# A graph layer's edge kernel on one core: second layer's units behind the repeat, gates reordered, node table in three pieces, start and end written out

## The reference

```
r    = edge_vec / |edge_vec|                                      # 3 numbers; sh1 = sqrt(3) * r
xs, xd = x[src], x[dst]                                           # gather
s1 = 16 scalars, v1 = 16 vectors of both
w  = relu(emb @ fc1_w1 / sqrt(10)) @ fc1_w2 / 4                   # 512 weights of this edge
s_t, v_t = tensor product of (s1, v1, sh1) with w                 # 8 scalars, 8 vectors
w2 = relu(emb @ fc2_w1 / sqrt(10)) @ fc2_w2 / 4                   # 384 weights of this edge
scal, gates, vecs = tensor product of (s_t, v_t, sh1) with w2
edge_out = [tanh(scal), vecs * tanh(gates)] * norm                # 32 numbers
```

## Time and profile before

| what | us |
|---|---|
| median of 3 runs (784.5 to 785.16) | 785.0 |
| the profiled execution | 785.59 |
| its span, first to last instruction | 783.4 |
| VectorE busy | 728.3 (93%) |
| TensorE busy | 672.7 (86%) |
| ScalarE busy | 552.9 (71%) |
| GpSimd busy | 536.4 (68%) |
| largest group: L728 x104, 2290 ns each | 238.2 |
| next: L690 x104, 2289 ns each | 238.1 |

### The profile page before, as it was taken

The page is one execution under the profiler, slowest core; times in us unless marked ns, Lnnn a source line. Parts: engine busy times, 40 slices in busy tenths (PEclk is TensorE's granted clock), DMA queues, the critical chain, the costliest instruction groups (busy, mean ns, idle before and its releaser), DMA issues.

```text
span 783.4 us, 20601 instructions
## 1 busy us (share of the span) xinstructions
PE 672.7 (86%) x6667; PEld 306.0 (39%) x6770; DVE 728.3 (93%) x1321; ACT 552.9 (71%) x1279; POOL 536.4 (68%) x655
## 2 busy tenths in 40 slices
PE   0788889999998999899998999899999998999874
PEld 0533434443444444343444434344444434443323
DVE  8389999999999999999999999999999999999964
ACT  2267777777777777877787777777777777777731
POOL 8577877688767877687768776887688767876100
PEclk9699999999999999999999999999999999999998
DMA  3321111111111111111112111111111111111000
GB/s 103 92 61 21 45 28 38 24 43 27 39 28 44 28 25 37 44 28 28 40 24 44 26 39 24 47 28 39 21 45 28 34 28 37 27 25 24 11 1 22
DMA packets 36099, 27.34 MB, mean 35 GB/s; under 512 B 14326, under 2 KB 34448, under 8 KB 35994
## 3 DMA queue, kind: packets, MB, share of 16 engines
q1 hardware_dynamic: 21646, 18.15, 8.1%
q0 software_dynamic: 13312, 6.84, 5.9%
q10 hardware_dynamic: 1036, 1.02, 0.4%
HBM read 21.77 MB, written 4.20 MB: 33 GB/s over the span
## 4 chain that ended last, share of the span: by engine, by line
PE 60%; DVE 29%; issue 7%; DMA 1%; ACT 1%; POOL 0%; DVEq 0%; SPq 0%; POOLq 0%
DVE z_s L728 13%; PE ps L957 12%; PE ps L894 10%; PE ps L878 8%; DVE p_s L690 7%; PE ps L937 6%; PE ps L866 4%; PE ps L912 4%; PE ps L858 3%; PE ps L885 3%; PE ps L950 2%; PE ps L925 2%; PE ps L944 2%; PE ps L968 1%; DMA x_dram<-eo_all 1%
## 5 line engine op out<-in xcount | busy, mean ns | idle before, releaser
L335 POOL DMA_INDIRECT xs<-in_xp,src_i x416 | 405.4, 974 | 111.7 <-issue 105.5
L728 DVE TENSOR_TENSOR z_s<-ps,h 128x2048 f32<-128x2048 f32 x104 | 238.2, 2290 | 10.5 <-PE ps L912 1.2
L690 DVE TENSOR_TENSOR p_s<-ps,h 128x2048 f32<-128x2048 f32 x104 | 238.1, 2289 | 5.9 <-PE ps L957 5.9
L483 ACT CAST v_s<-ps 128x512 bf16<-128x512 f32 x312 | 181.4, 581 | 48.6 <-PE ps L878 45.3
L957 PE MATMUL ps<-f,w_f 32*128 32x512 f32 x832 | 120.5, 645 | 50.3 <-DVE z_s L728 32.0
L878 PE MATMUL ps<-p_s,sum_m 128*32 128x512 f32 x832 | 110.8, 601 | 15.3 <-DVE m L744 8.4
L894 PE MATMUL ps<-z_s,w_z 128*32 128x512 f32 x832 | 110.8, 605 | 3.8 <-DVE z_s L728 2.5
L446 ACT COPY oht<-ps 42x512 bf16<-42x512 bf16 x104 | 60.3, 580 | 68.6 <-PE ps L858 68.6
L377 POOL TENSOR_TENSOR along<-fe,r 128x192 f32<-128x192 f32 x104 | 58.6, 564 | 56.7 <-ACT fe L464 50.7
L452 ACT COPY f<-ps 128x512 f32<-128x512 f32 x104 | 61.0, 586 | 41.1 <-PE ps L866 41.1
L937 PEld LDWEIGHTS ps<-ident,u 128*128 128x128 f32 x416 | 43.6, 140 | 86.4 <-issue 86.4
(11 more groups left out here) (115 smaller groups left out, 890.8 us busy)
## 6 DMA issues: line engine op xcount, KB each, us to landing
emb<-e_dram SPq DMA_DIRECT2D x309, 30.0 KB
xs<-in_xp,src_i POOLq DMA_INDIRECT x416
e_dram<-e_part SPq DMA_DIRECT2D x7, 360.0 KB, 3.2
e_in<-in_emb SPq DMA_DIRECT2D x8, 240.0 KB
window<-x_dram SPq DMA_DIRECT2D x104, 7.9 KB
x_dram<-eo_all SPq DMA_DIRECT2D x1, 585.9 KB
eo_all<-in_vec_t SPq DMA_DIRECT2D x1, 528.0 KB, 3.6
xt_n<-in_xt SPq DMA_DIRECT2D x1, 400.0 KB, 3.7
```

Source lines behind the costliest of these rows:

```text
L335: nc.gpsimd.indirect_dma_start(xs_r[n][:, t, :], None, xp, bass.IndirectOffsetOnAxis(src_i[:, m * T + t:m * T + t + 1], axis=0)).then_inc( ...
L483: nc.scalar.copy(v_s[:], v_ps).then_inc(v_step, 1)
L690: nc.vector.tensor_tensor(p_s[:], ps[:, 0:4, :], h1_r[m % 2][:].unsqueeze(1).to_broadcast([128, 4, BE]), ALU.mult).then_inc(p_done, 1)
L728: nc.vector.tensor_tensor(z_s[:], ps[:, 0:4, :], h2_r[k % 3][:].unsqueeze(1).to_broadcast([128, 4, BE]), ALU.mult).then_inc(z_done, 1)
```

## The change

- Order on PE and ACT: hidden_2(i+1) at the end of step i becomes hidden_2(i) in step i, on PE behind repeat(i-1) and ahead of sum_1(i), on ACT first of all.
- `gates`: m4 first, then m1, then the addition to m4.
- Node table: `x_dram` is (3, N + 42, 32) instead of (N + 42, 96); each part is stored when ready, by a DMA of its own; a window load has 126 rows of 64 bytes instead of 42 of 192.
- Start: the misfits copy on DVE right after the first weight copy; turn_one_hot(0) one step earlier; the keep_warm(8) at i = -3 gone; tile 3 of block 1's and tile 0 of block 2's gather behind the branch on the flag.
- End: STEPS ends at NB; what remains of the last four blocks is written out. There over_nodes also waits for accumulate of the block before, and the keep_warm calls are 2, 4 and 4 instead of 4, 8, 8 and 4.

```diff
-        x_dram = nc.dram_tensor("x_dram", (N + WIN, PARTS * D), BF16, kind="Internal").ap()
+        x_dram = nc.dram_tensor("x_dram", (PARTS, N + WIN, D), BF16, kind="Internal").ap()
...
-        STEPS = range(-5, NB + 6)
+        STEPS = range(-5, NB + 1)
...
-                sp.dma_start(window_r[m % 3][:], x_dram[bass.ds(base, WIN), :].rearrange("m (n c) -> m n c", n=PARTS)
+                sp.dma_start(window_r[m % 3][:], x_dram[:, bass.ds(base, WIN), :].rearrange("n m c -> m n c")
                              ).then_inc(window_loaded[m % 3], 16)
...
-            sp.wait_ge(x_part_ready, PARTS)
-            sp.dma_start(x_dram[0:N, :].rearrange("(p m) c -> p m c", p=P), x_part.rearrange("p m n c -> p m (n c)")
-                         ).then_inc(x_stored, 16)
+            for n in range(PARTS):
+                sp.wait_ge(x_part_ready, n + 1)
+                sp.dma_start(x_dram[n, 0:N, :].rearrange("(p m) c -> p m c", p=P), x_part[:, n, :, :]).then_inc(x_stored, 16)
...
-            gather(1, 0, T)
-            gather(2, 0, 1)
+            gather(1, 0, 3)
             pool.wait_ge(r4_ready, 1)
             pool.wait_ge(misfits_ready, 1)
...
+                        if i == -4:
+                            gather(1, 3, T)
                         if real(i + 3):
                             directions(i + 3)
                         if i == -3:
-                            gather(2, 1, T)
+                            gather(2, 0, T)
...
             for i in STEPS:
+                if real(i):
+                    hidden_2(i)
                 if real(i):
                     part_of_v(i, 0)
...
                 if real(i - 4):
                     copy_one_hot(i - 4)
-                if real(i + 1):
-                    hidden_2(i + 1)
                 later_emb(i)
...
+            copy_one_hot(NB - 3)
+            tanhs(NB - 2)
+            copy_one_hot(NB - 2)
+            tanhs(NB - 1)
+            copy_one_hot(NB - 1)
...
             link(nc.vector.tensor_copy(w_first[:], w1_s))
+            dve.wait_ge(misfit_sum, 1)
+            nc.vector.tensor_copy(misfits[:], ps[0:1, 7, 0:1]).then_inc(misfits_ready, 1)
             link(nc.vector.tensor_tensor(w1_s, w1_s, w_first[:], ALU.subtract))
...
-                r = r4[:, T * k:T * k + T, :].unsqueeze(3).to_broadcast([128, T, 4, 16])
-                nc.vector.tensor_tensor(m1[:], e_ps[:, :, :, 0:16], r, ALU.mult).then_inc(fin_step, 1)
                 r = r4[:, T * k:T * k + T, 1:4].unsqueeze(3).to_broadcast([128, T, 3, 8])
                 nc.vector.tensor_tensor(m4[:], e_ps[:, :, 0:1, 16:24].to_broadcast([128, T, 3, 8]), r,
                                         ALU.mult).then_inc(vec_step, 1)
+                r = r4[:, T * k:T * k + T, :].unsqueeze(3).to_broadcast([128, T, 4, 16])
+                nc.vector.tensor_tensor(m1[:], e_ps[:, :, :, 0:16], r, ALU.mult).then_inc(fin_step, 1)
                 dve.wait_ge(vec_step, k + 1)
...
+            a, b, c, d = range(NB - 4, NB)
+            gates(c)
+            gated(b)
+            gate_sums(c)
+            outputs(b)
+            gates(d)
+            base = base_of(a)
+            gated(c)
+            gate_sums(d)
+            outputs(c)
+            accumulate(a, base)
+            base = base_of(b)
+            accumulate(b, base)
+            flag = dve.value_load(misfits[0:1, 0:1], min_val=0, max_val=EP)
+            gated(d)
+            outputs(d)
+            for k in (c, d):
+                base = base_of(k)
+                accumulate(k, base)
...
                 if k + 6 > NB:
                     pe.wait_ge(ohs_ready, k + 1)
+                    pe.wait_ge(acc_done, k)
...
             for i in STEPS:
+                if i == -4:
+                    turn_one_hot(0)
                 if real(i - 1):
                     repeat(i - 1)
+                if real(i):
+                    hidden_2(i)
                 if real(i):
                     sum_1(i)
...
                     misfits_of_all()
-                    keep_warm(8)
-                if i == -3:
                     keep_warm(8)
...
-                if real(i + 4):
+                if real(i + 4) and i + 4 >= 1:
                     turn_one_hot(i + 4)
...
-                if real(i + 1):
-                    hidden_2(i + 1)
-                if i == NB:
-                    flag = pe.value_load(misfits[0:1, 0:1], min_val=0, max_val=EP)
-                    nodes_themselves()
-                    keep_warm(4)
-                if i in (NB + 1, NB + 2):
-                    keep_warm(8)
-                if i == NB + 3:
-                    keep_warm(4)
+            keep_warm(2)
+            over_nodes(NB - 4)
+            turn(NB - 1)
+            flag = pe.value_load(misfits[0:1, 0:1], min_val=0, max_val=EP)
+            over_nodes(NB - 3)
+            nodes_themselves()
+            over_nodes(NB - 2)
+            keep_warm(4)
+            over_nodes(NB - 1)
+            keep_warm(4)
```

More of the change, by code:

```diff
@@ L73, in program @@
         w_z = sb("w_z", [128, 2, D])
-        no_rows = sb("no_rows", [WIN, PARTS * D], BF16)
+        no_rows = sb("no_rows", [WIN, PARTS, D], BF16)
         src_i = sb("src_i", [128, TILES], I32)
@@ L128, in program @@
         x_rest = early(P, NT * D).rearrange("p (m c) -> p m c", m=NT)
-        x_part = early(P, PARTS * NT * D // 2).bitcast(BF16).rearrange("p (m n c) -> p m n c", n=PARTS, m=NT)
+        x_part = early(P, PARTS * NT * D // 2).bitcast(BF16).rearrange("p (n m c) -> p n m c", n=PARTS, m=NT)
         vt = early(128, 3 * TILES).rearrange("p (e k) -> p e k", k=3)
@@ L291, in _ @@
             sp.wait_ge(zeroed, 1)
-            sp.dma_start(x_dram[N:N + WIN, :], no_rows[:]).then_inc(x_stored, 16)
-            sp.wait_ge(x_part_ready, PARTS)
-            sp.dma_start(x_dram[0:N, :].rearrange("(p m) c -> p m c", p=P), x_part.rearrange("p m n c -> p m (n c)")
-                         ).then_inc(x_stored, 16)
+            sp.dma_start(x_dram[:, N:N + WIN, :].rearrange("n m c -> m n c"), no_rows[:]).then_inc(x_stored, 16)
+            for n in range(PARTS):
+                sp.wait_ge(x_part_ready, n + 1)
+                sp.dma_start(x_dram[n, 0:N, :].rearrange("(p m) c -> p m c", p=P), x_part[:, n, :, :]).then_inc(x_stored, 16)
             sp.wait_ge(bases_loaded, 16)
-            sp.wait_ge(x_stored, 32)
+            sp.wait_ge(x_stored, 64)
             load_window(0)
@@ L525, in _ @@
                     act.wait_ge(x_rest_ready, n)
-                nc.scalar.copy(x_part[:, :, n, :], xt_s if n == 0 else x_rest).then_inc(x_part_ready, 1)
+                nc.scalar.copy(x_part[:, n, :, :], xt_s if n == 0 else x_rest).then_inc(x_part_ready, 1)
                 if n < 2:
@@ L592, in rest_of_x @@
                 dve.wait_ge(x_part_ready, n + 1)
-                nc.vector.tensor_tensor(x_rest, xt_s if n == 0 else x_rest, x_part[:, :, n, :], ALU.subtract).then_inc(x_rest_ready, 1)
+                nc.vector.tensor_tensor(x_rest, xt_s if n == 0 else x_rest, x_part[:, n, :, :], ALU.subtract).then_inc(x_rest_ready, 1)
             def directions(step, first, end):
@@ L660, in _ @@
                                            op1=ALU.add).then_inc(weights_ready, 1)
-            dve.wait_ge(misfit_sum, 1)
-            nc.vector.tensor_copy(misfits[:], ps[0:1, 7, 0:1]).then_inc(misfits_ready, 1)
             one_hot(3)
@@ L753, in _ @@
             for i in STEPS:
-                if i == NB + 4:
-                    flag = dve.value_load(misfits[0:1, 0:1], min_val=0, max_val=EP)
                 if real(i):
```

## The result

The changed kernel takes 761.52 us (median of 4 runs, 759.47 to 762.05) against 784.75 for the one before on the same chip: ratio 0.9702, 95% interval 0.9681 to 0.9723. The forecast was 756.5, range 747 to 769.

What follows compares the result with a forecast made beforehand. The prediction took a plain step to be bound by a loop over VectorE and PE (6.84 of 6.85 us). 785.59 - 24 (steps) - 2.4 (start) - 2.0 (end) = 757.2, median 0.6 lower, so 756.5; range 747 to 769.

Steps and rivals of the forecast that it cites:

- (a): Plain step, PE and ACT: hidden_2 moved behind repeat takes 0.31 us out of the two-engine loop, 6.84 to 6.53.
- Size of the step: Plain step: 6.56 us, from limits VectorE 6.50, loop 6.53 and PE's round 6.55; mean step 6.61 with the split.
- 0.07 at both seams: PE, L866 to L912 and L912 to L950: idle 0.07 at each change of shapes, giving a round of 6.69.
- PE takes the bound: Rival, steps: seams cost 0.07 to 0.14 or L495 delays the cast; mean step 6.74, total 769; chance 0.22.
- (b): VectorE's gates, m4 before m1: 0.78 to 0.67 us, saves 0.11 a step, VectorE alone 6.50; L728 starts at 0.60.
- The split's pair: Two steps in twelve, GpSimd and ScalarE splitting edge features: 0.6 us longer per pair from GpSimd colliding with VectorE, 0.05 a step.
- fits: ScalarE in the step: L495, 0.6 us long, can start near 0.95, before its cast of sum_1's result at 1.90.
- The start: Before the steps: table in three pieces brings Rows(0) 2.8 us earlier; 2.4 passed on through GpSimd (bounds 0 and 6).
- 6 us of moving: Table store at the start: the last third takes about 2 of the 6 us, landing about 3.2 us earlier.
- The end: Last four blocks, new order: last product starts at 769.2 instead of 771.19, -2.0 us (bounds 0 and -4).
- a granted clock at 1.2 GHz: Sign of a wrong forecast, TensorE: half clock beyond the slice now at 0.6; a PE round near 13 us.
- The slower rival: VectorE's small operations (L710 to L715) run into GpSimd every step, up to 0.45 us each; total 801; chance 0.05.

Runs made afterwards that it cites:

- undo_a_again: Changed kernel with hidden_2(i+1) back at the end of the step on PE and ACT, second run: 777.1 us, 0.9909 of the kernel before.
- undo_a: Changed kernel with hidden_2(i+1) back at the end of the step on PE and ACT, first run, on a longer chip: 0.996 of the kernel before.
- act_split: Changed kernel with ScalarE's two casts of the split behind hidden_2 of the next step, on a longer chip: 0.9687 of the kernel before.
- split_later: Changed kernel with ScalarE's split casts, nodes_themselves and a gather reordered, and GpSimd's split part one step later: 1029.65 us, 0.9825 of the kernel before.
- undo_b_again: Changed kernel with gates in the old order (m1, m4, addition), second run, on a longer chip: 0.9663 of the kernel before.

## Why the prediction was right, point by point

- *Place of the gain.* The loop L728, L957 to L866, L912 was named as the bound, and (a) as what shortens it; undo_a_again shows 15.4 of 16.7. Undoing the order of gates and the table together costs 1.1 in the same stretch.
- *Size of the step.* 6.56 forecast, 6.63 measured. The term that was wrong is the seam from turn_features straight to repeat: I took it at no cost and had only put "0.07 at both seams" into the rival. It costs 0.53 - 0.44 = 0.09, once, and inside the loop, where it counts fully: 6.53 + 0.09 = 6.62. The other seam, L940 to L978, is 0.33 where I had 0.47, but it lies outside the loop. PE's round of 6.55 was right: its pieces now add up to 6.56, with 0.07 idle.
- *The sum, and luck in it.* The 94 steps brought 5.9 less than forecast and the end 1.5 less; the start brought 2.2 more and the steps up to block 9 0.7 more. The whole was missed by only 5.0 because the start, mis-sized too, made up part of the loss: with the start as forecast the time would be near 764, outside the 751 to 763 that I gave as the forecast itself.
- *The rival "PE takes the bound"* came half true. Its sign is there, VectorE idle ahead of the former L728 (0.1 a step), and the mean step of 6.68 lies halfway between my 6.61 and its 6.74. One of its two seams cost 0.09; PE alone is still not the bound, the loop over both engines is.
- *The order of gates.* The 0.11 on VectorE is exact (6.50), its value in time 0.01 a step, because the loop binds. I had L728 start 0.60 behind the end of products by (b); it starts 0.71 behind, when repeat is through. The step of the sum did not rest on it.
- *The split's pair.* 0.6 for GpSimd's collision, 0.69 measured (6.98 + 6.97 - 2 x 6.63), right in size by luck and wrong in cause: the prediction's sentence that L495 "fits" held for plain steps only, and with the extra cast it did not.
- *The start.* 2.4 against 4.6. The last third was issued at 14.86 and landed at 18.5, not at 20: the first window's load is issued at 19.53, behind SP's load of the base, where it was at 24.24. No row shows my "6 us of moving" and the 3.2 earlier worked out from it; the runs show 3.6 from issue to landing for a third, 8.28 for the whole, and a landing 4.7 earlier. GpSimd passed on more than I let it: its first directions come 3.6 earlier (24.16 against 27.73) and those of block 3 4.6 (51.50 against 56.13).
- *The end.* 2.0 against 0.5. The sign "a granted clock at 1.2 GHz" came here: the clock fell twice, behind 2.37 and 2.20 of idle on PE, and once in the kernel before. sum_2 of the last block ran at the lower level (L921 1.93, 1.06 in the kernel before), and two groups of keep_warm, 1.2 and 1.1, stood ahead of the last product. At the clock of the old end the new one is some 1.6 to 1.9 shorter (undo_a, act_split), so the order of the work was worth what I said, and what I left out is that its idle on PE can cost the clock.
- *The slower rival*, collision in every step, did not come: L718's greatest duration in the changed kernel is 0.26. It stays confined to the split's steps, in the kernels named above.

## What to carry to other kernels

When a step is a loop over two engines, add it up from start-to-start distances and ask which work lies inside the loop and which can be done while the partner works; moving one short matmul behind the hand-over was worth 15.4 of the 16.7 us won in the steps here, and an exact saving on the busier engine next to nothing. Count the seam that a move creates as well as the work that it takes away. When a wait is removed and nothing is gained, look at once for what the wait had kept apart.

## What the runs showed of the hardware that was not expected

On three of the six chips that the experiments met, the kernel before took 1010.41, 1011.54 and 1047.73 us, 29 to 34% longer. The largest instruction lasts as long as elsewhere (the median of `products` is 2.285 to 2.292), but the median step is 8.57 to 8.90, and 9.39 in split_later, instead of 6.63 (6.85 in undo_a). The granted clock is lower over the whole execution (0.95 in the profiled one of undo_b_again, 0.98 in the changed kernel's), but that is not the cause: from 211.53 to 306.68 us undo_b_again had a granted clock of 1.00 and its steps still took 8.65 in the mean. Much of the time stands ahead of instructions, in waits that the profile puts down to "remote" and for which I found no releaser in the program; the changed kernel has none of these from 300 to 700 us. A wait of undo_b_again in that stretch (us in total, times, longest):

```profile
DVE acc L711 <- remote: 56.3, 34, 2.7
```

The last steps, with no gather and no window load left, run at 6.48 to 6.64 there too (6.51 to 6.85 in undo_a). What holds the instructions up was not found.
